# Edge keys fetched by 29 gathers on both halves of the partitions in place of 51 on one half, in a graph network on one core

## The reference

```python
h = relu(layernorm(x))
m = relu(concat(h[src], edge_attr) @ w1a + b1a) @ w1b + b1b
agg = segment_sum(m, dst) / max(count(dst), 1)
x = x + relu(concat(h, agg) @ w2a + b2a) @ w2b + b2b
f = feat0 = relu(layernorm(x))
for _ in range(10):
    agg = segment_sum((f * src_norm)[src], dst)
    f = 0.9 * agg * dst_norm + 0.1 * feat0
x = x + f
```

## Time and profile before

| | us |
|---|---|
| median of 3 runs | 6082.6 (6082.08 to 6087.5) |
| profiled execution, device time | 6090.69 |
| its span | 6088.8 |

### The profile page before, as it was taken

One profiled execution on the slowest core, in us unless ns is written; L12 is line 12 of the kernel. 1 busy time (PEld: TensorE's weight loads), 2 busy tenths in 40 slices (PEclk: granted clock), 3 DMA queues, 4 the chain that ended last, 5 costly groups with the idle time before them and its releaser, 6 DMA issues. The chain is left out here.

```text
span 6088.8 us, 196769 instructions
## 1 busy us (share of the span) xinstructions
PE 4983.6 (82%) x76542; PEld 3065.0 (50%) x76542; DVE 4011.7 (66%) x11958; ACT 788.4 (13%) x1725; POOL 4331.9 (71%) x4300
## 2 busy tenths in 40 slices
PE   1675656555666563999999999999999999999997
PEld 1564555545555542555555555555555555555554
DVE  7897777777677777656566565656556566665655
ACT  0343333333333310000000000000000000000000
POOL 5777777777777764775767767676776767677675
PEclk9987777777777776999999999999999999999999
DMA  4543333333333322656556555655656566565655
GB/s 129 129 120 97 100 94 95 97 98 98 96 95 95 95 52 98 208 197 208 196 205 213 198 204 200 208 197 206 208 197 206 200 212 207 198 205 192 215 196 176
DMA packets 530050, 980.41 MB, mean 161 GB/s; under 512 B 295963, under 2 KB 461307, under 8 KB 483147
## 3 DMA queue, kind: packets, MB, share of 16 engines
q1 hardware_dynamic: 377002, 841.91, 39.6%
q0 software_dynamic: 136864, 97.04, 9.4%
q10 hardware_dynamic: 15232, 28.37, 1.2%
HBM read 775.11 MB, written 204.68 MB: 161 GB/s over the span
## 5 line engine op out<-in xcount | busy, mean ns | idle before, releaser
L1798 POOL DMA_INDIRECT x_nodes_fast<-feature_rows,x_nodes_fast x2560 | 2619.0, 1023 | 1059.9 <-issue 873.7
L2103 PE MATMUL banks_fast<-count_units_fast,feature_parts_fast 128*32 128x512 fp8e3 x58848 | 3256.9, 380 | 50.3 <-DVE gathered_hots L1983 34.4
L2103 PEld LDWEIGHTS banks_fast<-count_units_fast,feature_parts_fast 128*32 128x32 bf16 x58848 | 1549.5, 97 | 1589.2 <-issue 61.6
L1917 DVE TENSOR_SCALAR count_units_fast<-packed_ring_fast 128x512 int32<-128x512 int32 x2459 | 1067.4, 434 | 1378.0 <-PE banks_fast L2103 1328.4
L146 POOL DMA_INDIRECT rows_fast<-row_table,idx_fast x1456 | 1428.2, 981 | 443.7 <-issue 415.7
L1918 DVE TENSOR_SCALAR count_units_fast<-packed_ring_fast 128x512 int32<-128x512 int32 x2459 | 1042.4, 424 | 0.0
L1225 DVE TENSOR_SCALAR window_place_hot_fast<-iota_wide_fast,local_keys_fast,target_weight_fast 128x196 bf16<-128x196 f16 x3136 | 953.1, 349 | 0.0
L1335 PE MATMUL banks_fast<-identity_fast,rows_fast 128*128 128x128 f32 x784 | 221.3, 375 | 670.1 <-DMA rows_fast<-row_table,idx_fast 667.8
L1318 PE MATMUL banks_fast<-window_place_hot_fast,window_src_hot_fast 128*128 128x196 bf16 x3136 | 611.5, 282 | 25.3 <-DVE window_place_hot_fast L1225 18.0
L1324 PE MATMUL banks_fast<-window_place_hot_fast,window_src_hot_fast 128*128 128x196 bf16 x3136 | 593.8, 276 | 0.0
L1335 PEld LDWEIGHTS banks_fast<-identity_fast,rows_fast 128*128 128x128 f32 x784 | 97.8, 175 | 722.9 <-DMA rows_fast<-row_table,idx_fast 590.9
(11 more groups left out here) (315 smaller groups left out, 2159.0 us busy)
## 6 DMA issues: line engine op xcount, KB each, us to landing
packed_ring_fast<-edge_counts SPq DMA_DIRECT2D x352, 1792.0 KB
edge_counts<-count_stage_fast SPq DMA_DIRECT2D x100, 784.0 KB
running_sums<-run_sums_fast SPq DMA_DIRECT2D x100, 768.0 KB
x_nodes_fast<-feature_rows,x_nodes_fast POOLq DMA_INDIRECT x2560
rows_fast<-row_table,idx_fast POOLq DMA_INDIRECT x1456
feature_rows<-feature_parts_fast ACTq DMA_DIRECT2D x50, 384.0 KB
rows_fast<-attrs_padded SPq DMA_DIRECT2D x98, 128.0 KB
attrs_padded<-in_edge_attr SPq DMA_DIRECT2D x1, 12500.0 KB, 44.7
```

The costliest lines, as they stand in the source:

```text
L1798: pool.indirect_dma_start(out=rows[:, g % GSLOTS, i, :], out_offset=None, in_=b.dram.feature_rows[side], in_offset=bass.IndirectOffsetOnAx ...
L1917: nc.vector.tensor_scalar(to[..., 0:P // 8], of, NIBBLES, None, ALU.bitwise_and)
L2103: last = nc.tensor.matmul(b.banks[at:at + DN, SWEEP[half_of(side, m)], 0:COLS], parts[:, side, j, k * DN:(k + 1) * DN], of_strip.bitcast(FP8),
```

## The change

One gather fetches the keys of two pairs: pair 2f on partitions 0 to 63, pair 2f+1 on partitions 64 to 127. A pass of the loop has seven pairs, so it needs four fetches (`KEY_FETCHES` = 4), the last of which has keys of pair 6 alone; its other half fetches from index 0 and nobody reads it. `window_row` becomes [128, 32], laid out as 4 columns for each pass, and `raw_keys` has 4 slots of 128 partitions. VectorE's copy of indices and GpSimd's fetch happen in pairs 1, 3, 5 and 6 instead of in every pair. Ahead of the loop stand four fetches instead of six. `turn_keys` picks its half through the columns of the identity matrix. In `prepare_sorted`, four matmuls and two copies replace two matmuls and one copy. The number of fetches is 4 + 4 x 6 + 1 = 29, where it was 6 + 7 x 6 + 3 = 51.

```diff
+KEY_FETCHES = (AHEAD_GROUPS + 1) // 2
 # prepare_sorted, VectorE
-            step(nc.vector.tensor_copy(window_row[:, 0:J // SLOTS], b.banks[0:SLOTS * WG, 2, 0:J // SLOTS]))
+            for half in range(2):
+                on = slice(half * SLOTS * WG, (half + 1) * SLOTS * WG)
+                by_loop = lambda t: t.rearrange("p (i f) -> p i f", f=KEY_FETCHES)[on, :, 0:KEY_FETCHES - half]
+                step(nc.vector.tensor_copy(by_loop(window_row[:, 0:J // BATCH * KEY_FETCHES]), by_loop(b.banks[:, 2, 0:J // BATCH * KEY_FETCHES])))
 # prepare_sorted, TensorE
-            for k in range(SLOTS):
-                last = nc.tensor.matmul(b.banks[0:SLOTS * WG, 2, 0:J // SLOTS], first_of[:, k, :],
...
+            for half in range(2):
...
+                for k in range(SLOTS):
+                    last = nc.tensor.matmul(of_half, first_of[:, k, :],
...
 # messages_and_counts
-        key_idx = sb("key_idx", [LW, AHEAD_GROUPS], I32)
-        raw_keys = sb("raw_keys", [P, AHEAD_GROUPS, P, 2])
+        key_idx = sb("key_idx", [2 * LW, KEY_FETCHES], I32)
+        raw_keys = sb("raw_keys", [2 * LW, KEY_FETCHES, P, 2])
+        fetch_behind = {pair: pair // 2 for pair in (*range(1, AHEAD_GROUPS, 2), AHEAD_GROUPS - 1)}
 # GpSimd, a step
-                if t % SLOTS:
-                    pool.wait_ge(keys_pointed, k + 1)
+                if t % SLOTS and t // SLOTS in fetch_behind:
+                    r_keys = fetch_behind[t // SLOTS]
+                    pool.wait_ge(keys_pointed, i * KEY_FETCHES + (r_keys + 2))
                     pool.sem_inc(taken, 1)
-                    fetch_keys((t // SLOTS + KEYS_AHEAD) % AHEAD_GROUPS)
+                    fetch_keys(r_keys)
 # GpSimd, ahead of the loop
-            for r in range(KEYS_AHEAD):
+            for r in range(KEY_FETCHES):
                 fetch_keys(r)
 # VectorE, at a pair's start
-                        nc.vector.tensor_copy(key_idx[:, r_keys:r_keys + 1], window_row[:, bass.ds(k + AHEAD_GROUPS, 1)]).then_inc(keys_pointed, 1)
+                        if t // SLOTS in fetch_behind:
+                            r_keys = fetch_behind[t // SLOTS]
+                            nc.vector.tensor_copy(key_idx[:, r_keys:r_keys + 1],
+                                                  window_row[:, bass.ds((i + 1) * KEY_FETCHES + r_keys, 1)]).then_inc(keys_pointed, 1)
 # TensorE
-            def turn_keys(r):
+            def turn_keys(pair):
+                r, half = divmod(pair, 2)
...
-                                            b.ident[:, 0:LW], start=True, stop=True, skip_group_check=True)
+                                            b.ident[:, half * LW:(half + 1) * LW], start=True, stop=True, skip_group_check=True)
...
-                            pe.wait_ge(keys_in[next_keys % AHEAD_GROUPS], (i + next_keys // AHEAD_GROUPS + 1) * 16)
+                            pe.wait_ge(keys_in[next_keys % AHEAD_GROUPS // 2], (i + next_keys // AHEAD_GROUPS + 1) * 16)
```

More of the change, by code:

```diff
@@ L1011, in _ @@
             pe.wait_ge(counted, 1)
-            for k in range(SLOTS):
-                last = nc.tensor.matmul(b.banks[0:SLOTS * WG, 2, 0:J // SLOTS], first_of[:, k, :],
-                                        start[:, :].rearrange("p (i s) -> p s i", s=SLOTS)[:, k, :],
-                                        start=(k == 0), stop=(k == SLOTS - 1))
+            for half in range(2):
+                on = slice(half * SLOTS * WG, (half + 1) * SLOTS * WG)
+                of_half = b.banks[on, 2, 0:J // BATCH * KEY_FETCHES].rearrange("p (i f) -> p i f", f=KEY_FETCHES)[:, :, 0:KEY_FETCHES - half]
+                for k in range(SLOTS):
+                    last = nc.tensor.matmul(of_half, first_of[:, k, :],
+                                            start[:, :].rearrange("p (i a s) -> p s i a", a=AHEAD_GROUPS, s=SLOTS)[:, k, :, half::2],
+                                            start=(k == 0), stop=(k == SLOTS - 1))
             last.then_inc(summed, 1)
@@ L1032, in messages_and_counts @@
         attrs_in = [sem(f"attrs_in{r}") for r in range(AHEAD_GROUPS)]
-        keys_in = [sem(f"keys_in{r}") for r in range(AHEAD_GROUPS)]
+        keys_in = [sem(f"keys_in{r}") for r in range(KEY_FETCHES)]
         sums_out = [sem(f"sums_out{s}") for s in range(SLOTS)]
@@ L1063, in messages_and_counts @@
         n_loops, PAIRS_A_LOOP = J // BATCH, BATCH // SLOTS
-        KEYS_AHEAD, ATTRS_AHEAD = AHEAD_GROUPS - 1, AHEAD_GROUPS - SLOTS
+        ATTRS_AHEAD = AHEAD_GROUPS - SLOTS
+        fetch_behind = {pair: pair // 2 for pair in (*range(1, AHEAD_GROUPS, 2), AHEAD_GROUPS - 1)}
         KEY_STEPS, RUN_STEPS = 6, G + 1
@@ L1075, in fetch_keys @@
             def fetch_keys(r):
-                pool.indirect_dma_start(out=raw_keys[0:LW, r, :, :].rearrange("p e k -> p (e k)"), out_offset=None,
+                pool.indirect_dma_start(out=raw_keys[:, r, :, :].rearrange("p e k -> p (e k)"), out_offset=None,
                                         in_=b.dram.keys.rearrange("e (k a) -> (e k) a", a=1),
@@ L1174, in _ @@
             dve.wait_ge(filled, FILLS)
-            nc.vector.tensor_copy(key_idx[:, :], window_row[:, 0:AHEAD_GROUPS]).then_inc(keys_pointed, 1)
+            nc.vector.tensor_copy(key_idx[:, :], window_row[:, 0:KEY_FETCHES]).then_inc(keys_pointed, 1)
             dve.sem_inc(hot, SLOTS * WG)
@@ L1194, in _ @@
                     g, k, s, r = i * BATCH + t, i * PAIRS_A_LOOP + t // SLOTS, t % SLOTS, t % AHEAD_GROUPS
-                    r_keys = t // SLOTS
                     if s == 0:
@@ L2224, in fast_way @@
             same, cont, last_row, tail = sb("same_target", [P, G + T]), sb("run_goes_on", [P, 1]), sb("last_row", [P, J]), sb("last_sums", [P, DH])
-            window_row = edge_ctx.enter_context(nc.sbuf_tensor("window_row", [SLOTS * WG, J // SLOTS + AHEAD_GROUPS], I32))
+            window_row = edge_ctx.enter_context(nc.sbuf_tensor("window_row", [2 * SLOTS * WG, (J // BATCH + 1) * KEY_FETCHES], I32))
             out_int = edge_ctx.enter_context(nc.sbuf_tensor("out_int_fast", [P, 2, WC], I32))
```

## The result

The changed kernel took 6052.49 us in the median of 5 runs (6043.97 to 6053.09), the kernel before 6082.08 in 5 (6078.45 to 6087.5): ratio 0.9947, 95% interval 0.9934 to 0.9961. That is 29.6 us by the medians and 32 by the ratio (24 to 40 by its interval), where 25.5 were forecast. The two profiled executions differ by more, 6090.69 against 6052.81. The median lies in the stated range (6050 to 6068), and the direction and the price of a fetch held, but something that the sum held fixed moved: the profiled execution was forecast at 6065.2 us and took 12.4 less.

What follows compares the result with a forecast made beforehand. GpSimd's unbroken stream of gathers was taken as the bound: 62.6 us of key gathers out, 37.1 in, a gain of 25.5, so 6082.6 - 25.5 = 6057.1 us, range 6050 to 6068.

Steps and rivals of the forecast that it cites:

- the price of a fetch: GpSimd: a 128-partition key gather costs a row gather's 0.944 us ahead of the loop, 0.981 in it, plus 0.305 pause.
- What bounds the stage: GpSimd issues gathers end to end and sets the stage's end; TensorE follows with about 8 us of slack a group.
- What goes, what comes: GpSimd's stream: 51 key gathers, 62.6 us with pauses, go; 29 wide ones, 37.1 us, come; gain 25.5 us.
- A: Key gathers: partitions cost their share, a wide one costs two narrow; gain 0.3 us, time 6082.3; chance 0.05.
- C: Something other than GpSimd's stream ends last, so about half the gain comes through: 6069.9 us; chance 0.05.
- B: VectorE stretches wide key gathers to 3.98 us each: 61.7 us more, time 6144.3; chance 0.02.
- What else moves: Side effects outside the key gathers' price: nothing gained or lost, GpSimd stays the bound, later stages start 25.5 us earlier.
- late keys: Possible new wait for keys in the loop: about 82 us of lead against landing of 5.4 us at most; nobody waits.
- `prepare_sorted`: Its end gets two more matmuls and one more copy, finished before 155.0 us; cost nothing, 1 us at most uncovered.
- the later stages: Stages behind GpSimd's gather stage keep their length and start 25.5 us earlier.
- The first keys' landing: Key gathers land in 2.6 us median, 5.4 at most; with twice the bytes perhaps twice that, and nobody waits.

Runs made afterwards that it cites:

- first pair: The kernel before and the changed kernel, as first profiled: profiled executions 6090.69 and 6052.81 us.
- the second: The kernel before and the changed kernel, both unedited, run and profiled again: 6084.31 and 6053.55 us.
- comparisons by window: Both kernels with VectorE's 128x1024 two-tensor comparison replaced by 8 comparisons of 128 columns with a scalar: changed kernel 6033.75 us, kernel before 6058.16.
- the cut in four: Both kernels with VectorE's 128x1024 one-hot instruction cut into four of 128x256: changed kernel 6057.95 us, kernel before 6083.02.
- moving the fetches: Changed kernel with each key fetch in the loop issued behind the eighth row gather of its step, not ahead of the first: 6047.97 us.

## Why the prediction was right, and where it was wrong

- **What bounds the stage.** Right. GpSimd's stream has no idle time but the pauses, and TensorE follows it 1.3 us behind. Stream and span shrink together: by 39.4 and 37.6 us in the first pair, by 27.4 (2148.45 to 2121.04) and 23.0 in the second.
- **What goes, what comes.** Right. 62.6 us went out, 37.2 came in, and 37.1 were forecast. A wide fetch costs 0.980 us, where 0.976 was taken in the mean; the width alone cost 0.05 us a fetch, near the 0.04 that the medians had shown. With its pause a fetch is 1.285 us; issuing 29 more cost 1.25 us each, and leaving 25 out of the loop shortened GpSimd's stream by 32.5 us (2102.84 to 2070.30), 1.30 each. Rivals A and C are out, and so is B as it was priced: no wide fetch of the changed kernel took more than 1.04 us (29 x 2.155 in its sum is 62.5, not 62.6, which decides nothing).
- **What else moves.** Right as to late keys (one wait, at the start), `prepare_sorted` and the later stages (3934.5 us behind GpSimd's last row gather before, 3936.3 after; over the profiles of all runs this varies from 3929.5 to 3936.3). The first keys' landing rose to 6.9 us and cost nothing.
- **The failed step: the sum held the 1456 row gathers at the 1428.2 us that they took before.** It has a term for key gathers alone, and gives no reason why the row gathers should keep their price across two programs and two executions. In the profiled pair they took 13.9 us less, so GpSimd's last one started at 2113.92 us, not near 2128; in the second pair they took 2.3 us less. Most of their excess over 0.944 us (43.1 of 53.7 us) isn't a property of a gather but of how many begin while L1221 runs, and it was the part that moved (to 29.6). The prediction had this cause in its hands as rival B, that GpSimd can be "held up by what VectorE does". It dismissed it with "VectorE's instructions there are short" and the maximum of 1.50 us, instead of asking what the 0.04 us between mean and median sums to over 1456 gathers. That the median still lies in the range is partly luck: its low end has room for the spread of the runs (5.4 us) and a cheaper fetch, and none for row gathers.
- **What stays open.** How much of the surplus over 25.4 us belongs to the change. It is 4.2 us by the first medians, 5.4 by the second (6084.31 to 6053.55), about 7 by the ratios, whose intervals reach from 24 to 41 us. The changed kernel's row gathers were lower in both profiles, by 8.1 us in the mean, but one kernel varies by 6 itself. With comparisons by window the surplus is gone (24.4). That fits a change that shifts which gathers meet L1221, but isn't proof: the cut in four left the stretch and showed 25.1, and moving the fetches moved nothing clearly.

## What to carry to other kernels

Where GpSimd's stream of gathers is the bound, as here, count the gathers, not their bytes: one gather of 128 partitions x 1 KB in place of two of 64 saved 1.2 us. A mean above the median in such a stream is a sum worth naming before it is held fixed, since neighbours can make it, as VectorE's comparison did here. Beside such a stream it can pay to try small VectorE instructions that read one SBUF tensor in place of a large one that reads two, as long as VectorE has the time: here it took 16 us off.

## What the runs showed of the hardware

- A gather to 128 partitions takes 0.944 us in the median with 128 B a partition and 0.96 to 1.00 in the mean with 1 KB, holds included; one to 64 partitions with 1 KB takes 0.91 to 0.93. The pause between two gathers is 0.305 us.
- A 128x1024 bf16 comparison of two SBUF tensors (0.68 us) holds a gather that begins in its first 200 ns by 0.43 us; two of them back to back hold one that begins in the first 100 ns by 0.97 us in the mean. VectorE's own duration doesn't change (684 ns). The Trainium skill says, in "SBUF — State Buffer", section "Who interferes with whom", that an instruction of VectorE with two SBUF inputs contends with one of GpSimd that reads SBUF; that a gather counts as one, since its indices lie in SBUF, is my reading. The runs agree with it: leaving the instruction out took the stretch from 45.2 to 9.1 us. The same section says that a `tensor_tensor` was seen not to stall a DMA's issue, and infers that descriptor generation needs only the other, the write side; for these gathers the runs show otherwise. Replacing it by comparisons with one SBUF tensor each left 28.1 us, and how much of that gain is due to the missing input no run here tells.
- Cutting such an instruction into four back to back doesn't free the gathers: 41.4 us of stretch against the changed kernel's 39.8 and 45.2.
